# Moving the transposes of the feed-forward part from SP's queue to ACT's, and the quantiser's work tile from PSUM to SBUF

## The reference

```python
def fp4_quant_dequant(x):            # along the last dim, blocks of 16
    scale = max(abs(xb)) / 6.0       # at least 1e-12
    idx = searchsorted([0.25, 0.75, 1.25, 1.75, 2.5, 3.5, 5.0], abs(xb / scale))
    return [0.0, 0.5, 1.0, 1.5, 2.0, 3.0, 4.0, 6.0][idx] * sign(xb) * scale
def fp4_linear(x, w):                # x @ w.T with both rounded
    return einsum('bsk,nk->bsn', fp4_quant_dequant(x), fp4_quant_dequant(w))

x = x + attention(layernorm(x))
n = layernorm(x)
h = silu(fp4_linear(n, w_gate)) * fp4_linear(n, w_up)
x = x + fp4_linear(h, w_down)
```

## Time and profile before

| | |
|---|---|
| time, median of 3 runs | 10486.58 us (10485.94 to 10522.72) |
| the profiled execution | 10500.62 us, span of its slowest core 10498.9 us |
| spans of the 8 cores | 10457.2 to 10498.9 us |
| busy: DVE, PE, ACT, POOL | 5859.3, 4150.8, 1476.8, 239.4 us |
| rounding of the weights | 0 to about 1100 us |
| attention | to about 4735 us |
| weights transposed | 4735 to about 4841 us |
| the 16 feed-forward chunks | from there to the end, about 353 us each |

### The profile page before, as it was taken

The page is one execution under the profiler, slowest core; times in us unless marked ns, Lnnn a source line. Parts: engine busy times, 40 slices in busy tenths (PEclk is TensorE's granted clock), DMA queues, the critical chain, the costliest instruction groups (busy, mean ns, idle before and its releaser), DMA issues.

```text
span 10498.9 us, 60787 instructions; the slowest of 8 cores (10457.2 to 10498.9 us)
## 1 busy us (share of the span) xinstructions
PE 4150.8 (40%) x18030; PEld 1767.1 (17%) x18304; DVE 5859.3 (56%) x6821; ACT 1476.8 (14%) x2262; POOL 239.4 (2%) x445
## 2 busy tenths in 40 slices
PE   0000354555545555442444444443444334434433
PEld 0000122222222222111111111111111111111211
DVE  8999444543444433453476447545754575457445
ACT  0000222333223332320000000000000000000000
POOL 0000000000000000000000000000000000000000
PEclk9999866666667666665766666666667667666766
DMA  3111111111111111104101110111011101110110
GB/s 73 44 45 54 45 47 44 37 48 42 47 43 38 44 43 47 46 23 82 39 19 32 37 39 17 33 38 39 15 33 40 40 14 34 39 40 13 35 37 30
DMA packets 547589, 408.86 MB, mean 39 GB/s; under 512 B 479424, under 2 KB 479424, under 8 KB 546240
## 3 DMA queue, kind: packets, MB, share of 16 engines
q1 hardware_dynamic: 495392, 215.66, 8.6%
q0 software_dynamic: 51872, 189.30, 4.8%
HBM read 118.56 MB, written 180.88 MB: 29 GB/s over the span
## 4 chain that ended last, share of the span: by engine, by line
DVE 47%; DMA 16%; PE 16%; DVEq 6%; SPq 6%; issue 6%; ACT 2%; ACTq 0%; POOLq 0%; PEldq 0%; POOL 0%
DVE bfar L283 10%; DVE bfar L276 10%; DMA bfar<-hqs 9%; DVE ps L267 3%; DVE ps L270 3%; DVE bfar L272 3%; DVE far L259 3%; DVEq L287 3%; PE ps L548 3%; PE ps L669 3%; DVE bfar L292 3%; PE ps L502 2%; DMA hqs<-bfar 2%; PE ps L557 2%; DVE bfar L841 2%
## 5 line engine op out<-in xcount | busy, mean ns | idle before, releaser
L502 PE MATMUL ps<-bfar 128*128 128x512 bf16 x3009 | 781.3, 423 | 2326.8 <-DMA bfar<-xn1s 1895.7
L283 DVE SCALAR_TENSOR_TENSOR bfar<-ps,bfar 128x1024 bf16<-128x1024 f32 (+2 forms) x1232 | 1500.5, 1218 | 96.5 <-issue 5.1
L827 PE MATMUL ps<-bfar 128*128 128x512 bf16 (+1 forms) x3011 | 807.0, 438 | 1332.3 <-ACT bfar L816 1326.3
L889 PE MATMUL ps<-bfar 128*128 128x512 bf16 x2759 | 736.8, 415 | 1210.8 <-DMA bfar<-hqs 1206.9
L804 PE MATMUL ps<-bfar 128*128 128x512 bf16 (+1 forms) x3011 | 798.9, 435 | 958.9 <-DMA bfar<-xqs 734.9
L276 DVE SCALAR_TENSOR_TENSOR bfar<-ps,bfar 128x1024 bf16<-128x1024 f32 (+2 forms) x924 | 1125.5, 1218 | 72.4 <-issue 3.9
L502 PEld LDWEIGHTS ps<-bfar 128*128 128x128 bf16 x3072 | 323.1, 107 | 2784.5 <-issue 2500.7
L909 DVE TENSOR_TENSOR far<-far,ps 128x1024 f32<-128x1024 f32 x64 | 78.2, 1221 | 1251.5 <-PE ps L889 1073.2
L841 DVE TENSOR_TENSOR bfar<-ps,bfar 128x2816 bf16<-128x2816 f32 x64 | 197.9, 3092 | 1031.6 <-PE ps L827 832.3
L252 ACT ACTIVATE bfar<-bfar 128x1024 bf16<-128x1024 bf16 (+1 forms) x192 | 189.1, 985 | 3264.8 <-DVE bfar L292 2148.6
L827 PEld LDWEIGHTS ps<-bfar 128*128 128x128 bf16 x3072 | 345.3, 114 | 1794.0 <-issue 1695.5
(11 more groups left out here) (68 smaller groups left out, 3790.0 us busy)
## 6 DMA issues: line engine op xcount, KB each, us to landing
hqs<-bfar POOLq DMA_DIRECT2D x64, 704.0 KB, 3.4
far<-x SPq DMA_DIRECT2D x64, 512.0 KB, 5.9
x1s<-far POOLq DMA_DIRECT2D x64, 512.0 KB, 2.9
far<-x1s SPq DMA_DIRECT2D x64, 512.0 KB, 7.5
out<-far POOLq DMA_DIRECT2D x64, 512.0 KB, 3.0
xn1s<-bfar POOLq DMA_DIRECT2D x64, 256.0 KB, 2.3
aos<-bfar POOLq DMA_DIRECT2D x64, 256.0 KB, 2.3
xqs<-bfar POOLq DMA_DIRECT2D x64, 256.0 KB, 2.3
```

The lines of the kernel that those rows point to most:

```text
L283: e.scalar_tensor_tensor(out=g, in0=u, scalar=t, in1=g, op0=ALU.is_gt, op1=ALU.add)
L502: last = e.matmul(ps[:, col:col + 512], lhs_fn(k), rhs_fn(k), start=(k == 0), stop=(k == 7))
L827: last = e.matmul(ps[:, ns:ns + nw], bfv(F_XQT + k * CHUNK + t * 128, [[1, 128]]), bfv(WUQ + k * FI + ns, [[1, nw]]), start=(k == 0), stop ...
L889: last = e.matmul(ps[:, PS_DN + t * DM + half * 512: PS_DN + t * DM + half * 512 + 512], bfv(F_HQT + sl * 512 + t * 128, [[1, 128]]), bfv( ...
```

## The change

Four edits, all in the feed-forward part. The transposes of the weights, of `xqs` and of `hqs` are issued from ACT's queue in place of SP's, with their waits unchanged. The quantiser of the feed-forward part keeps `u` in `far`, behind the two buffers in which `v_res` writes. The first down product waits for the fourth tile's `v_h` in place of its last rounding step (it waits for the transpose of the stored result as before).

```diff
-        p.on("sync", p2_w)
+        p.on("scalar", p2_w)
...
-            p.on("sync", l_xqt)
+            p.on("scalar", l_xqt)
...
                         bfv(F_H + qoff, [[16, Fs // 16], [1, 16]]),
-                        Fs, uoff=PS_QU, nboff=qoff // 16)
+                        Fs, usb=X_SB + 4096 + 2048, nboff=qoff // 16)
...
             hq_done = sG.n
-            vlast = sV.n
+            vlast = vh_inc[0]
...
-                p.on("sync", l_hqt)
+                p.on("scalar", l_hqt)
```

## The result

| | before | changed |
|---|---|---|
| median of 8 runs | 10491.03 us | 10184.14 us |
| lowest and highest | 10481.41, 10522.72 | 10159.18, 10221.93 |
| spans of the profiled execution's cores | 10457.2 to 10498.9 | 10119.2 to 10201.5 |

The changed kernel is 307 us faster, ratio 0.9703 (95% interval 0.9686 to 0.9720). The prediction was 337 us, 10150, with a range of 10085 to 10250; it forecast the right direction and the range holds the time.

The account below looks back on a forecast made before the run. The prediction took the chain of waits, not a busy engine, as the bound, with the tile loop bound by DVE and its store. 243 + 94 = 337 us off 10486.6 gave 10150, range 10085 to 10250.

Parts of the forecast that it names:

- Part A: Between chunks: xqs transposes on ACT no longer wait behind v_res and loads; 243 us gained, between 211 and 265.
- stores later: Chunk boundary: three stores that v_res waits for take 0.5 us more each beside the transposes; 22 us lost, at most 54.
- Part B: Feed-forward quantiser: u in SBUF speeds line 272 to 693 and 558 ns; 94 us gained, lower bound 73.
- Part C: 352 hqs and 38 weight transposes issued from ACT at SP's pace: 0 gained, 35 us either way.
- The rival in which the stores take the gain back: v_res between chunks: three stores each land 5.9 us later, only the 94 us from u remain, 10393; chance 0.05.
- rival of slow issue: Chain of 22 hqs transposes: an ACT issue takes 2.24 us, not 1.12; 533 us slower, 10683; chance 0.06.
- Part D: Earlier release of the down product: 0 us, since PE waits there for the first hqs transpose.
- quantiser without gain: Line 272 stays at 1225 ns or other readers of u slow; only 243 us gained, 10244; chance 0.06.
- cheaper SBUF reads: Quantiser's nine readers of u take 65 ns less each; 112 us more gained, 10038; chance 0.03.

Follow-up runs that it names:

- Experiment 3: Changed kernel with all transposes back on SP's queue, those of xqs ahead of the x1s loads: 10171.09 us, ratio 0.9695.
- experiment 4: Changed kernel with the down product waiting for the last rounding step again: 10168.94 us, ratio 0.9695.
- experiment 6: Changed kernel with two further loads of 512 KB behind the four of x1s in each chunk: 10233.97 us, ratio 0.9719.
- experiment 9: Changed kernel with residual addition in place, xqs transposes issued early, and hqs transposes no longer waiting for one another: 9708.18 us, ratio 0.9187.

## Why the prediction was right, and where its sizes were off

The mechanism was the forecast one, and the sizes were off by 30 us. On core 7 the gain of the span is 10490.9 - 10201.5 = 289.4 us, and it comes apart along the prediction's parts:

| | forecast | core 7 | from |
|---|---|---|---|
| A, `xqs` past the wait | +243 | +229 | 719.7 - 217.9 - 272.7 |
| of it, stores later | -22 | -26 | 178.8 to 204.5 |
| B, `u` in SBUF | +94 | +96 | line 272: 128 x 0.531 + 64 x 0.398; 3 from lines 267 and 270 |
| C, the `hqs` chain from ACT | 0, within 35 | -31 | 1074.5 to 1105.4 |
| A, B and C together | +337 | +294 | |

The remaining 4 us lie ahead of the chunks, where the weights' transposes ended 4 us later.

**Part A** went as described: the wait in SP's queue is gone, `v_res` is late next, the transposes are there in time. The forecast store delay of 0.5 us each was 25.7 / 48 = 0.54. Experiment 3 shows that the reason given (the order of the queue, not the engine) is the right one. The rival in which the stores take the gain back had the right mechanism at a tenth of its price. One piece of the working is wrong without effect: a landing is counted from the start of an issue, so n transposes in a row take n - 1 steps and one landing. The 22 of the earlier trace rows then take 60.2 us and not 58.67 + 2.6 = 61.3 (7295.56 + 2.6 = 7298.2, when the last product starts), and the eight of `xqs` would land at 7308.7 at the earliest and not at 7309.9. The same slip makes the rival of slow issue some 33 us too dear.

**Part B** was right to 2 us in 94. In the earlier trace rows the slope between the small instructions of line 262 gave 684 ns and line 288 had 693, and 694 came. The rule of fixed costs in the Trainium skill (VectorE: DVE Perf Modes, The TRN2 errata) would, by the prediction's estimate, have taken 65 ns off lines 276 and 283 too; they stayed at 1225.

**Part C** is the term that was mis-sized, by 31 us on the slowest core. That is within the 35 us that the prediction allowed it, but for a reason that it did not name. On cores 0, 1, 2, 4 and 6 it came out as forecast: 1069.6 to 1079.5 us. Cores 3, 5 and 7 had 1099.7 to 1105.4; in the kernel before no core had over 1083.6. The prediction priced ACT's issue, and experiment 3 clears ACT: SP has it too. What it did not price is that cores of a pair drift apart. Core 7 issued its last loads of `x1s` at 9869.6 and core 6 at 9815.5, each counted from its own start, although their first came 1 us apart (4856.3 and 4855.2); in the kernel before, the last were 4 us apart (10134.7 and 10130.5). Most of these 54 us are the longer chain itself (33.5 us more on core 7 than on core 6) and the longer waits for stores (16.8), so the drift is in part its effect. But some of it comes first. Through the first six chunks core 7 waits only 5 us more for the chain than core 6 and falls 18 us behind; in the ten after them it waits 29 us more. In experiment 3 core 0 is 27 us behind core 1 from the first chunk on, and its chain is long in nearly all. What of a neighbour's traffic then meets the chain was not settled: with one load in four no long chain was seen in 16 cores, with six loads it did not grow. That the lag is the cause is not shown either; no run set it.

**Part D** was right: experiment 4 shows no difference beyond its interval. The rivals with a quantiser without gain, cheaper SBUF reads and slow issue are each refuted by a row: 694, 1225 and 1124 ns.

The forecast's own arithmetic also took the gain of one core for the gain of the slowest: core 4 gained 10498.9 - 10123.0 = 376 us, but the time is that of core 7, which gained 289. On core 4, whose rows the forecast used, A gave 734.9 - 223.1 - 258.0 = 254, B 96 and C -1.5, 349 us beside the 337. The other 27 are none of its terms: 11 lie ahead of the chunks (the last weight transpose was issued at 4823.8 in place of 4834.7), and about 14 in the gate and up products of each chunk's first tile, which were shorter (the core's granted clock was 0.704 before and 0.718 after). So a part of the fit of any one core is chance.

## What to carry to other kernels

Look at what a DMA stands behind in its queue before asking which engine should issue it: here a transpose whose data and buffer were free stood 20 us behind a load that waited for something else, and reordering one queue was worth as much as using a second. When such a wait goes, name what is late next and go on from there: the additions' waits for their stores, then the time of the transposes, then the one-by-one chain, which together were worth more than the change itself. Where a work tile moves out of PSUM, count the instructions that read one tensor and constants: here they gave 93 of 96 us.

## What the runs showed of the hardware that was not expected

- With transposes beside them the stores of a core are late, and in most pairs of cores more so on the odd one. In the first profile of the changed kernel the waits for stores are 187.7 to 193.7 us on even cores and 203.5 to 212.1 on odd ones; before they were 174.3 to 178.8 on all. With one load in four the two groups stay apart (189.6 to 191.7 and 196.8 to 204.0), so the other three loads are not needed for it. It is up to one us a chunk. One pair, cores 0 and 1 of experiment 6, had no difference (197.5 and 197.8).
- A DMA transpose of `hqs` took 16 ns more to issue from ACT than from SP on every core, and 15 ns more on even cores than on odd ones: 1139 and 1123 ns on even, 1124 and 1108 on odd. The median landing was 2.6 us from either. In the changed kernel's first profile the cores with a long chain are also those with the longest single landing: 5.1 to 5.3 us on cores 3, 5 and 7, at most 4.1 on the others.
- Once PE bounds a stretch, its length follows the granted clock: in one profile of experiment 9 the down product of a chunk took 40.75 us at 0.94 in the mean and 48.34 at 0.78, a ratio of 1.19 beside 1.21 of the clocks.
